# Which C products GpSimd makes, chosen for each core stage: fourteen in the first, nine, eight, then seven, five in the last

## The reference

```python
def step(h, t):
    u_t, d_t, B_t, C_t = t
    dA = jnp.exp(d_t[:, :, None] * A)
    h = dA * h + (d_t * u_t)[:, :, None] * B_t[:, None, :]
    y_t = jnp.einsum('bdn,bn->bd', h, C_t)
    return (h, y_t)
...
y = ys.transpose(1, 0, 2) + u_c * Dp
y = y * jax.nn.silu(res)
```

## Time and profile before

| | us |
|---|---|
| median of three runs | 1926.14 |
| profiled execution, own time | 1929.45 |
| span in the profile | 1927.7 |
| GpSimd busy: gathers (1024) | 991.8 |
| GpSimd busy: C products (112) | 264.5 |
| DVE busy: scans (256) | 582.9 |
| DVE busy: feeds (256) | 313.4 |
| DVE busy: C products (144) | 174.8 |
| ScalarE busy: copies to c_row (112) | 65.3 |
| TensorE busy: sums of the products (1024 matmuls) | 487.0 |

### The profile page before, as it was taken

The page is one execution under the profiler, slowest core; times in us unless marked ns, Lnnn a source line. Parts: engine busy times, 40 slices in busy tenths (PEclk is TensorE's granted clock), DMA queues, the critical chain, the costliest instruction groups (busy, mean ns, idle before and its releaser), DMA issues. The chain is left out here.

```text
span 1927.7 us, 24488 instructions
## 1 busy us (share of the span) xinstructions
PE 1567.3 (81%) x5953; PEld 852.3 (44%) x6042; DVE 1678.5 (87%) x4332; ACT 1484.2 (77%) x3129; POOL 1367.8 (71%) x1209
## 2 busy tenths in 40 slices
PE   5788787979898989999898989899898988776340
PEld 2333444535454545455454545454554545343120
DVE  3979888899999999999999999999999998944554
ACT  5656687869898988898898989998898977664330
POOL 0433737288887787878778877877788776877766
PEclk8889899999999999999999999999999999896555
DMA  6110202022323323232323232232323222333333
GB/s 153 55 39 28 71 24 75 22 78 83 96 85 88 90 69 103 75 101 83 95 82 97 85 89 86 71 110 72 95 85 99 81 87 76 89 110 99 98 93 93
DMA packets 84508, 159.43 MB, mean 83 GB/s; under 512 B 21096, under 2 KB 47104, under 8 KB 84288
## 3 DMA queue, kind: packets, MB, share of 16 engines
q0 software_dynamic: 49152, 134.28, 24.1%
q1 hardware_dynamic: 33952, 23.04, 4.0%
q10 hardware_dynamic: 1248, 0.34, 0.1%
HBM read 149.20 MB, written 8.39 MB: 82 GB/s over the span
## 5 line engine op out<-in xcount | busy, mean ns | idle before, releaser
L1518 POOL DMA_INDIRECT rows<-in_experts,index x1024 | 991.8, 969 | 335.2 <-issue 291.6
L1396 DVE TENSOR_TENSOR_SCAN hp<-dA,fed_ps 128x1024 f32<-128x1024 f32 x256 | 582.9, 2277 | 4.5 <-issue 1.4
L805 PE MATMUL ysum<-hp,ident 128*128 128x512 f32 x1024 | 487.0, 620 | 6.1 <-DVE hp L1406 3.0
L1533 POOL TENSOR_TENSOR hp<-hp,c_row 128x1024 f32<-128x1024 f32 x112 | 264.5, 2361 | 165.5 <-ACT c_row L1069 131.8
L1380 DVE TENSOR_TENSOR fed_ps<-du,b_ps 128x1024 f32<-128x1024 f32 x256 | 313.4, 1224 | 43.0 <-PE b_ps L780 31.2
L1052 ACT ACTIVATE dA<-delta,decay 128x511 f32<-128x511 f32 x512 | 333.1, 711 | 11.1 <-issue 4.8
L805 PEld LDWEIGHTS ysum<-hp,ident 128*128 128x128 f32 x1024 | 205.3, 201 | 224.9 <-issue 200.8
L1031 ACT ACTIVATE rows<-rows,coef 128x128 f32<-128x128 f32 x896 | 272.9, 393 | 6.3 <-DVE coef L1299 6.3
L955 ACT ACT_TABLE_LOAD x207 | 265.6, 1283 | 8.6 <-PEq L555 5.0
L1292 DVE CUSTOM_DVE_ANT_0 rows<-rows,xn 128x128 f32<-128x128 f32 x1024 | 227.4, 285 | 34.3 <-DMA rows<-in_experts,index 33.7
L738 PE MATMUL bank<-rows,ident 128*128 128x256 f32 x896 | 206.7, 384 | 0.7
(11 more groups left out here) (183 smaller groups left out, 2197.8 us busy)
## 6 DMA issues: line engine op xcount, KB each, us to landing
rows<-in_experts,index POOLq DMA_INDIRECT x1024, 2.7
x_in<-in_x SPq DMA_DIRECT2D x16, 256.0 KB, 4.1
rows<-in_x SPq DMA_DIRECT2D x16, 256.0 KB, 4.9
x_shifted<-rows SPq DMA_DIRECT2D x16, 256.0 KB, 2.0
x_res<-x_shifted SPq DMA_DIRECT2D x16, 256.0 KB, 4.4
y<-x SPq DMA_DIRECT2D x16, 256.0 KB, 2.6
rows<-in_taps SPq DMA_DIRECT2D x1, 512.0 KB
rows<-in_wq_t SPq DMA_DIRECT2D x1, 512.0 KB, 5.4
```

Source lines behind the costliest of these rows:

```text
L805: mm = nc.tensor.matmul(ysum[:, j, :], ident[:], hp[:, BUFFER[k], j, :], start=(k == SUM_ORDER[0]), stop=(k == SUM_ORDER[-1]))
L1396: nc.vector.tensor_tensor_scan(flat, dA[:, n % NDA, :, :].rearrange("p a b -> p (a b)"), fed_ps[:].rearrange("p a b -> p (a b)"), 0.0, ALU ...
L1518: pool.indirect_dma_start(e.rows[:, t, h, :], None, A["experts"], bass.IndirectOffsetOnAxis(ap=e.index[:, t, h:h + 1], axis=0)).then_inc(e ...
L1533: pool.tensor_tensor(state, state, c_row[:, k % NCR, :].unsqueeze(1).to_broadcast([P, NH, T]), ALU.mult).then_inc(pool_read, 1)
```

## The change

The set of states that GpSimd multiplies depends on the batch. Batch 0 has states 1 to 14, batch 1 has 1, 3, 4, 5, 7, 8, 9, 11, 13, batch 2 has 1, 3, 5, 7, 8, 9, 11, 13, batch 15 has 1, 3, 5, 7, 9, and the others keep the seven. So 120 products are on GpSimd in place of 112, and 136 on DVE in place of 144. The counts that the waits compare with, and the order of the sums (`sum_at`, `sum_order`), follow the set. In batch 0 TensorE so sums one state in each slot group instead of two in every other. c_row still has one row, and no piece has another slot.

```diff
-DVE_STATES = tuple(n for n in range(NS) if n not in POOL_STATES)
-
-SUM_AT = [min(n + 1 + (n in POOL_STATES), NS - 1) for n in range(NS)]
-SUM_ORDER = sorted(range(NS), key=lambda n: (SUM_AT[n], n))
...
+POOL_AT = {0: (1, 2, 3, 4, 5, 6, 7, 8, 9, 10, 11, 12, 13, 14), 1: (1, 3, 4, 5, 7, 8, 9, 11, 13), 2: (1, 3, 5, 7, 8, 9, 11, 13), 15: (1, 3, 5, 7, 9)}
+def on_pool(c):
+    return POOL_AT.get(c, POOL_STATES) if isinstance(c, int) else POOL_STATES
+def pool_count(c, n):
+    if isinstance(c, int):
+        earlier = sum(len(on_pool(k)) for k in range(c))
+    else:
+        earlier = c * len(POOL_STATES) + sum(len(on_pool(k)) - len(POOL_STATES) for k in range(LOOP_FROM))
+    return earlier + sum(k <= n for k in on_pool(c))
...
+def sum_at(c, n):
+    return min(n + 1 + (n in on_pool(c)), NS - 1)
+def sum_order(c):
+    return sorted(range(NS), key=lambda n: (sum_at(c, n), n))
...
-            if n in POOL_STATES:
-                return pool_read, at(c, len(POOL_STATES), POOL_STATES.index(n))
-            return read_out, at(c, len(DVE_STATES), DVE_STATES.index(n))
+            if n in on_pool(c):
+                return pool_read, pool_count(c, n)
+            return read_out, dve_count(c, n)
...
-                        for k in [x for x in SUM_ORDER if SUM_AT[x] == n]:
+                        order = sum_order(c)
+                        for k in [x for x in order if sum_at(c, x) == n]:
...
-                            if k >= NCR:
-                                act.wait_ge(pool_read, at(c, len(POOL_STATES), k - NCR))
-                            elif later(c):
-                                act.wait_ge(pool_read, at(c - 1, len(POOL_STATES), len(POOL_STATES) + k - NCR))
-                            nc.scalar.activation(c_row[:, k % NCR, :], c_ps[:, 0, :],
+                            if later(c) or n > on_pool(c)[0]:
+                                act.wait_ge(pool_read, pool_count(c, n) - NCR)
+                            nc.scalar.activation(c_row[:, 0, :], c_ps[:, 0, :],
...
-                    if CORE in has and part == 2 and n in DVE_STATES:
+                    if CORE in has and part == 2 and n not in on_pool(b[CORE]):
...
-                    if CORE in has and part == 0 and n in POOL_STATES:
-                        c, k = b[CORE], POOL_STATES.index(n)
+                    if CORE in has and part == 0 and n in on_pool(b[CORE]):
+                        c = b[CORE]
                         pool.wait_ge(scanned, at(c, NS, n))
-                        pool.wait_ge(c_kept, at(c, len(POOL_STATES), k))
+                        pool.wait_ge(c_kept, pool_count(c, n))
```

More of the change, by code:

```diff
@@ L223, with dve_count, summed @@
 POOL_STATES = (1, 3, 5, 7, 9, 11, 13)
-DVE_STATES = tuple(n for n in range(NS) if n not in POOL_STATES)
-SUM_AT = [min(n + 1 + (n in POOL_STATES), NS - 1) for n in range(NS)]
-SUM_ORDER = sorted(range(NS), key=lambda n: (SUM_AT[n], n))
-def summed(n):
-    return SUM_ORDER.index(n)
+POOL_AT = {0: (1, 2, 3, 4, 5, 6, 7, 8, 9, 10, 11, 12, 13, 14), 1: (1, 3, 4, 5, 7, 8, 9, 11, 13), 2: (1, 3, 5, 7, 8, 9, 11, 13), 15: (1, 3, 5, 7, 9)}
[7 more added lines that the diff above has]
+    return earlier + sum(k <= n for k in on_pool(c))
+def dve_count(c, n):
+    if isinstance(c, int):
+        earlier = sum(NS - len(on_pool(k)) for k in range(c))
+    else:
+        earlier = c * (NS - len(POOL_STATES)) + sum(len(POOL_STATES) - len(on_pool(k)) for k in range(LOOP_FROM))
+    return earlier + sum(k not in on_pool(c) for k in range(n + 1))
+def sum_at(c, n):
+    return min(n + 1 + (n in on_pool(c)), NS - 1)
+def sum_order(c):
+    return sorted(range(NS), key=lambda n: (sum_at(c, n), n))
+def summed(c, n):
+    return sum_order(c).index(n)
 def offset(phase, slot):
@@ L615, in multiplied @@
         def multiplied(c, n):
-            if n in POOL_STATES:
-                return pool_read, at(c, len(POOL_STATES), POOL_STATES.index(n))
-            return read_out, at(c, len(DVE_STATES), DVE_STATES.index(n))
+            if n in on_pool(c):
+                return pool_read, pool_count(c, n)
+            return read_out, dve_count(c, n)
         def c_used(c, n):
-            if n in POOL_STATES:
-                return c_kept, at(c, len(POOL_STATES), POOL_STATES.index(n))
+            if n in on_pool(c):
+                return c_kept, pool_count(c, n)
             return multiplied(c, n)
@@ L805, in iteration @@
                                 mm = nc.tensor.matmul(ysum[:, j, :], ident[:], hp[:, BUFFER[k], j, :],
-                                                      start=(k == SUM_ORDER[0]), stop=(k == SUM_ORDER[-1]))
+                                                      start=(k == order[0]), stop=(k == order[-1]))
                             mm.then_inc(y_sum, 1)
@@ L1060, in iteration @@
                             decays_of(k)
-                        if n in POOL_STATES:
-                            c, k = b[CORE], POOL_STATES.index(n)
+                        if n in on_pool(b[CORE]):
+                            c = b[CORE]
                             act.wait_ge(c_spread, at(c, NS, n))
-                            if k >= NCR:
-                                act.wait_ge(pool_read, at(c, len(POOL_STATES), k - NCR))
-                            elif later(c):
-                                act.wait_ge(pool_read, at(c - 1, len(POOL_STATES), len(POOL_STATES) + k - NCR))
-                            nc.scalar.activation(c_row[:, k % NCR, :], c_ps[:, 0, :],
+                            if later(c) or n > on_pool(c)[0]:
+                                act.wait_ge(pool_read, pool_count(c, n) - NCR)
+                            nc.scalar.activation(c_row[:, 0, :], c_ps[:, 0, :],
                                                  ACT.Copy).then_inc(c_kept, 1)
@@ L1392, in iteration @@
                         if before:
-                            dve.wait_ge(y_sum, at(c, NS, summed(before[-1])))
+                            dve.wait_ge(y_sum, at(c, NS, summed(c, before[-1])))
                         elif later(c):
-                            dve.wait_ge(y_sum, at(c - 1, NS, summed(max(k for k in range(NS) if BUFFER[k] == BUFFER[n]))))
+                            last = max(k for k in range(NS) if BUFFER[k] == BUFFER[n])
+                            dve.wait_ge(y_sum, at(c - 1, NS, summed(c - 1, last)))
                         nc.vector.tensor_tensor_scan(flat, dA[:, n % NDA, :, :].rearrange("p a b -> p (a b)"),
@@ L1527, in iteration @@
                     n, part = divmod(slot, TURN // NS)
-                    if CORE in has and part == 0 and n in POOL_STATES:
-                        c, k = b[CORE], POOL_STATES.index(n)
+                    if CORE in has and part == 0 and n in on_pool(b[CORE]):
+                        c = b[CORE]
                         pool.wait_ge(scanned, at(c, NS, n))
-                        pool.wait_ge(c_kept, at(c, len(POOL_STATES), k))
+                        pool.wait_ge(c_kept, pool_count(c, n))
                         state = hp[:, BUFFER[n], :, :]
                         pool.tensor_tensor(state, state,
-                                           c_row[:, k % NCR, :].unsqueeze(1).to_broadcast([P, NH, T]),
+                                           c_row[:, 0, :].unsqueeze(1).to_broadcast([P, NH, T]),
                                            ALU.mult).then_inc(pool_read, 1)
```

## The result

The kernel after takes 1945.12 us (median of four runs, 1942.36 to 1945.77), the one before in the same comparison 1923.28 (1916.88 to 1926.36): ratio 1.0113, 95% interval 1.0085 to 1.0140. The forecast was 1923, the range 1913 to 1931. The change is slower, by more than twice the 0.5% that a measurement can tell, and the time lies outside the range. The profiled execution of after took 1945.3 us, its span is 1943.6: 15.9 more than the span of before. Between the medians it is 21.8; the profiled execution of before, at 1929.45 us, was a long one, so the pair of profiles shows less than the whole loss.

The account below looks back on a forecast made before the run. DVE was taken as busiest (87%), with GpSimd spare in early cores and none in the last. Terms -2.5 - 1.9 - 0.3 + 1.5 = -3.2 us gave 1926.2 profiled, 1923 us as median; range 1913 to 1931.

Parts of the forecast that it names:

- should only shift in time: Cores 3 to 14 keep their seven states, so the change was taken to move them in time only, with no term.
- Core 0: Scans of batch 0: seven more products on GpSimd give 1.6 to 3.5 us, taken as 2.5.
- The walk: Four queues followed in program order through core 0: product 14 ends near 115.9, feed near 120.0, or 121.9 with low clock.
- Cores 1 and 2: Scans of batches 1 and 2: two products and one moved to GpSimd, gains of 1.9 us and 0.3 us.
- Core 15: Scans of batch 15: two products back on DVE make its end later, +1.5 us, between 0.5 and 2.3.
- The forecast's gap on GpSimd: In the tail, GpSimd waits 6 to 9 us instead of 2.7 between fetches of batch 15, first layer, and 13, second.
- the forecast's 4.5 us: In core 15's GpSimd queue, two fewer products at 2.24 us each put GpSimd 4.5 us ahead, then spent waiting.
- (1): Core 0 runs at DVE's pace, ACT never late: gain there 9 to 11.5 us, total 1914 to 1916.4; chance 0.17.
- (2): Tail is paid by GpSimd, not core 15's end: -4.5 in place of +1.5 us, total 1917; chance 0.13.
- (3): GpSimd's chain closes core 0 late, ACT's c_row copies falling behind each add: +5.6 us, 1931.7; chance 0.09.
- (4): GpSimd's products hold up DVE in cores 0 to 2: 23.6 us, about 1945; chance 0.03.
- The rule that was weighed: A DVE instruction with two SBUF inputs and a GpSimd instruction reading SBUF exclude each other; said to add nothing in core 0.

Follow-up runs that it names:

- 792: Kernel before with 16 more instructions (32 waits) ahead of ScalarE's loop, 792 in all: 1938.04 us, ratio 1.0072.
- 796: Kernel after, 796 instructions ahead of ScalarE's loop: 1945.12 us, ratio 1.0113. Also kernel before with 20 more there: 1947.37 us, ratio 1.0091.
- 820: Kernel after with 24 more instructions ahead of ScalarE's loop: whole change 1927.07 us, ratio 1.0017; with core 15's old set 1919.67 us, ratio 0.9979.
- 798: Kernel after with core 15's old set and two more instructions ahead of ScalarE's loop: 1922.93 us, ratio 0.9985 against before.
- 776: Kernel before unchanged, 776 instructions ahead of ScalarE's loop: 1923.28 us in the comparison with the kernel after.
- 844: Kernel after with core 15's old set and 48 more instructions ahead of ScalarE's loop: 1920.88 us, ratio 0.9979 against before.
- 868: Kernel after with core 15's old set and 72 more instructions ahead of ScalarE's loop: 1921.76 us, ratio 0.9995 against before.
- 892: Kernel after with core 15's old set and 96 more instructions ahead of ScalarE's loop: 1922.01 us, ratio 0.9981 against before.
- 904: Kernel after, whole change, with 108 more instructions (216 waits) ahead of ScalarE's loop: 1927.64 us, ratio 1.0014 against before.

## Why the prediction was wrong, by its own steps

**The step that failed** is the last sentence of its first paragraph but for four words: cores 5 to 14 "should only shift in time". It costs an edit at nothing without naming what hides it. What was edited are not the loop's instructions but their place, and that was worth +18.5 us in the pair of profiles, nearly six times the whole sum. None of the four rivals had it; the slower ones were about GpSimd's queue and DVE's operands. The trace of before held the hint: 1.02 to 1.53 us of idle time put down to "issue" ahead of the first dA of cores 7, 9, 11 and 13 and of no other core of the loop, a price of the jump that could turn out higher. The prediction read no timeline of the loop.

The rows show the mechanism. After the branch the first piece of the loop's code arrives: the move runs 2.4 to 3.1 us behind the branch in every kernel, half of it beside the table load, and 0.8 to 1.2 us after the end of the first packet. The next piece can be used, in the versions at 792 and 796 where its coming can be seen, only 4.4 to 7.2 us after the table load, 1.2 to 2.1 us after the end of the second packet, and ScalarE needs it when the first piece is used up. Where that holds the eight dA, 5.0 us of work, the second piece comes in time or nearly so. Where it ends after two instructions, all of the delay is seen. That these packets carry ScalarE's code is argued from their timing. Why the second comes so late isn't known. The Trainium skill, page Runtime: NRT & Kernel Launch, section Instruction fetch mechanics, says that a taken branch whose target isn't in the current window of two blocks forces a fetch before execution goes on; the rows agree. It gives blocks of 16 KiB; the packet in the hole is on a queue whose 104 packets moved 0.85 MB, 8 KB each.

**Core 0** came as walked. These are GpSimd's products 11 to 14 and the next batch's delta, in the kernel after, and DVE's feed at the end of the core:

```profile
98.08 2.36 POOL L1563 TENSOR_TENSOR hp<-hp,c_row 128x1024 f32<-128x1024 f32 x1 [2.50 <-ACT c_row L1098]
...
101.62 2.37 POOL L1563 TENSOR_TENSOR hp<-hp,c_row 128x1024 f32<-128x1024 f32 x1
103.93 2.35 POOL L1579 TENSOR_TENSOR delta<-delta,du 128x1024 f32<-128x1024 f32 x1
106.36 2.35 POOL L1583 TENSOR_TENSOR du<-delta,ucs 128x1024 f32<-128x1024 f32 x1
...
109.89 2.34 POOL L1563 TENSOR_TENSOR hp<-hp,c_row 128x1024 f32<-128x1024 f32 x1
...
113.41 2.36 POOL L1563 TENSOR_TENSOR hp<-hp,c_row 128x1024 f32<-128x1024 f32 x1
...
113.62 1.22 DVE L1436 TENSOR_TENSOR hp<-hp,c_ps 128x1024 f32<-128x1024 f32 x1 [3.09 <-PE c_ps L819]
121.77 1.23 DVE L1409 TENSOR_TENSOR fed_ps<-du,b_ps 128x1024 f32<-128x1024 f32 x1 [6.93 <-PE b_ps L810]
```

The walk had product 11 at 98.0, product 12 at 101.6, delta and du from 104.0 to 108.7, product 13 at 110.0, the end of 14 at 115.9 (it is 115.77) and the feed at 120.0, or 121.9 with a low clock (it is 121.77, against 123.50 in the earlier trace rows). The granted clock was indeed low there, 0.50, which is 1.2 GHz:

```profile
112.20:118.80 6.60, 5.82 (x8) 2.64 (x9) 1.22 (x1) 6.42 (x8) 6.03 (x5) 0.50 0.22 81
```

But that the last step hit to 0.1 us is luck: 7.01 for 5.40 us in the earlier trace rows makes the feed 121.1 to 121.6, not 121.9. DVE waits 6.93 us at the feed, not 8, as 3.09 us of its wait stand ahead of the product of state 15. In this pair of profiles the core is 1.6 us shorter (78.2 for 79.8). One pair can't tell it to a microsecond: with the new set the core is 75.9 to 78.2 us in nine profiles, and with the old one 76.8 to 79.8 in five.

**Cores 1 and 2**: core 1 88.9 us for 90.1 (-1.1, forecast -1.9), core 2 99.4 for 99.3 (forecast -0.3); core 3, with nothing changed, 101.9 for 103.5. The stretch up to core 5 gave -4.4, and -4.7 was forecast for cores 0 to 2; that these agree is luck, as 1.6 of the 4.4 are core 3's, which takes 101.9 to 104.4 us with either set. From core 0 to core 5 it is 471.7 to 475.8 us in the nine profiles with the new sets (mean 472.8) and 471.0 to 476.7 in the five with the old one (mean 475.0). By the ratios of the five versions without core 15's set, the three sets give 0.05 to 0.21%, 1.0 to 4.0 us.

**Core 15**: the sign was right, the size was not, and the pair of profiles hides it. The gate multiply ended 116.2 us after the core's first scan instead of 114.5, 1.7 later, as forecast. But in the other kernels with seven products it ends anywhere from 113.2 to 119.5, and with five from 116.2 to 117.3. What is common lies behind it: from the end of the gate multiply to the end of the kernel it is 231.3 to 232.7 us in all five profiles with five products, and 227.9 to 229.4 in seven of the nine with seven (231.3 in before, 232.0 at 792). TensorE's granted clock goes with it: in the 40 us from 40 us after the gate multiply its mean is 0.59 to 0.64 in the seven longer ones and 0.70 in the seven others. These are the windows of the whole change at 820 and of the version without core 15's set at 798:

```profile
1734.80:1774.80 40.00, 24.81 (x80) 14.50 (x79) 20.22 (x102) 15.71 (x42) 26.79 (x27) 0.59 0.28 80
```

```profile
1732.70:1772.70 40.00, 24.34 (x87) 14.89 (x86) 20.26 (x102) 17.33 (x44) 28.61 (x29) 0.70 0.33 91
```

A mean of 0.59 instead of 0.70 says that the clock fell from 2.4 to 1.2 GHz earlier in this stretch, in which TensorE's work for the expert code stands between DVE's steps. Core 15's set alone has 0.60, the version at 820 without it 0.70; before (0.64) and 792 (0.62) have seven products and go with the longer ones. Why it falls earlier with five products wasn't tried, and since before and 792 have an early fall too, that the set causes it is not shown; nor is it shown whether the clock makes the tail longer. The forecast's gap on GpSimd, 6 to 9 us between the fetches of batch 15 and 13, was sized wrongly as well: it is 4.58 where it was 2.72.

```profile
1694.23 0.94 POOL L1548 DMA_INDIRECT rows<-in_experts,index  x1 [3.84 <-issue]
1696.03 0.95 POOL L1548 DMA_INDIRECT rows<-in_experts,index  x1 [0.85 <-issue]
...
1753.23 0.94 POOL L1548 DMA_INDIRECT rows<-in_experts,index  x1 [2.21 <-DVE index L1312]
...
1772.10 1.07 POOL L1548 DMA_INDIRECT rows<-in_experts,index  x1 [0.30 <-issue]
1777.74 0.94 POOL L1548 DMA_INDIRECT rows<-in_experts,index  x1 [4.58 <-issue]
```

These rows show where the 4.5 us of the two products went. GpSimd is done with batch 15's fetches 177.2 us after the first scan of core 15, and in before it was 177.2 too (1759.12 less 1581.9): it got there no earlier. With two products less it waited on the way, 3.84, 0.85 and 2.21 us, where before had about 0.30 between fetches. So the forecast's 4.5 us ahead of the gap never came. Nor is the queue that runs without a pause, from which the forecast took them, typical: in seven of the nine profiles with seven products it also waits near the end of core 15, at first 1.1 to 2.4 us, and GpSimd reaches the gap after 175.6 to 180.5 us with seven products and after 177.1 to 178.2 with five. What ends the first two waits the trace doesn't say.

**The rivals**: (1) fell, ScalarE was late where the walk had it. (2) fell with core 15's set alone being slower. (3) fell, product 14 ended at 115.77, not after 119.4; its price of 1931.7 also lay outside the range that was said to take in most of it. (4) fell: the scans' mean is unchanged, 2278 ns for 2277. That its price of 1945 us is the time that was measured is chance, and the price doesn't come out of its own sum either: 1926.1 + 23.6 is 1949.7, with the gains gone. The rule that was weighed (the Trainium skill, page SBUF — State Buffer, section Who interferes with whom) neither cost nor gave anything that shows there, as the forecast had it: the longest of the 256 scans took 2290 ns, and the longest feed 1230.

## What to carry to other kernels

An edit ahead of a loop moves the loop in the engine's instruction stream; count the instructions of each engine ahead of every loop, before and after, as one counts the work. In the trace, look at the first instruction behind each jump back: idle time there with no releaser can be code that hasn't come. The sequencer's rows tell: when a few instructions run, then none, then the next, move the loop: two instructions more took 20 us out of it here (1077.8 to 1057.6). Do that before judging an edit: this one looked 1.1% slower, its work is 0.2% slower, and its better part at most 0.05 to 0.2% faster.

## What the runs showed of the hardware that I had not expected

- ScalarE's jump back costs 1.0 to 1.7 us of idle time behind a table load of 1.28 us in every cheap place (776, 798, 820, 844, 868, 892, 904 instructions ahead), and 4.6 to 7.2 us in the dear one (796); at 792 it costs 1.2 and a second hole of 1.9 to 3.4.
- The dear place is a matter of single instructions: 796 is dear, 798 cheap. How often such an edge comes along the stream was not tried.
- A hole of 3.3 to 5.1 us on ScalarE, whose busy share is 77%, was paid in full by the kernel: 16.6 us of holes, 18.5 us more of loop than in before, and at 792 11.5 for 11.5 (against the other cheap loops, which are shorter than that of before, it is more).
- GpSimd's and DVE's loops, moved by 20 and 236 instructions, cost nothing in the loop (1056.5 us); one shift of each was tried.
